# First stage of a four-layer network by groups: inputs, statistics and roots per group, rows turned one group ahead, two buffers of parts, first head's loads inside the stage

## The reference, cut to what matters

```python
xn = layernorm(x)                                   # no weights
q1, k1, q2, k2, v = split(xn @ Wqkv)                # 128, 128, 128, 128, 256 columns: 16 heads of 8 (v: 16)
lam = exp(lambda_q1 . lambda_k1) - exp(lambda_q2 . lambda_k2) + LAMBDA_INIT
diff = causal_softmax(q1, k1) @ v - lam * (causal_softmax(q2, k2) @ v)
x = x + layernorm(scaled_rms(diff) @ Wproj)
```

## Time and profile before

| | us |
|---|---|
| median of 3 runs | 1789.22 (1786.18 to 1791.82) |
| the profiled execution's own time | 1788.79 |
| its span, first to last instruction | 1787.0 |
| mean granted TensorE clock over the span | 0.943 |
| busy: PE, DVE, ACT, POOL | 1519.5, 1288.3, 1088.8, 1095.8 |

### The profile page before, as it was taken

One profiled execution on the slowest core, in us unless ns is written; L12 is line 12 of the kernel. 1 busy time (PEld: TensorE's weight loads), 2 busy tenths in 40 slices (PEclk: granted clock), 3 DMA queues, 4 the chain that ended last, 5 costly groups with the idle time before them and its releaser, 6 DMA issues. The chain is left out here.

```text
span 1787.0 us, 30008 instructions
## 1 busy us (share of the span) xinstructions
PE 1519.5 (85%) x8532; PEld 1025.8 (57%) x8532; DVE 1288.3 (72%) x3447; ACT 1088.8 (61%) x2348; POOL 1095.8 (61%) x1272
## 2 busy tenths in 40 slices
PE   3759999999999836468874899999999999988898
PEld 2413434344443315356653688888788888867565
DVE  5458887888888313755255899999999999983443
ACT  1105666676666721211312799999999999995242
POOL 5211565665647563104234699999999999974353
PEclk9958999999999968789986999999999999999899
DMA  3321011010100001762010000000000000000000
GB/s 118 113 64 36 22 26 29 19 36 18 30 24 20 2 1 47 246 225 95 1 47 0 1 1 2 1 1 1 1 1 1 29 21 1 1 1 1 1 24 24
DMA packets 39162, 59.48 MB, mean 33 GB/s; under 512 B 8700, under 2 KB 33160, under 8 KB 38152
## 3 DMA queue, kind: packets, MB, share of 16 engines
q1 hardware_dynamic: 39048, 58.12, 10.2%
HBM read 40.93 MB, written 16.78 MB: 32 GB/s over the span
## 5 line engine op out<-in xcount | busy, mean ns | idle before, releaser
L1896 POOL TENSOR_SCALAR c_R<-c_Z,c_negtau 128x256 f32<-128x256 f32 x519 | 589.7, 1167 | 51.4 <-DVE c_negtau L1965 29.7
L588 ACT ACTIVATE a_PT<-a_sc 128x512 f32<-128x512 f32 x576 | 318.4, 600 | 209.6 <-PE a_sc L653 207.2
L1851 ACT ACTIVATE c_R<-c_Z,c_negtau 128x256 f32<-128x256 f32 x1017 | 425.9, 517 | 3.5 <-DVE c_negtau L1998 1.8
L493 DVE TENSOR_REDUCE a_mpart<-a_nat 128x1 f32<-128x512 f32 (+3 forms) x640 | 364.0, 628 | 86.3 <-PE a_nat L620 48.1
L1932 DVE BATCH_NORM_STATS2 c_stat<-c_R 128x6 f32<-128x512 f32 x576 | 380.9, 678 | 1.7 <-ACT c_R L1851 1.6
L617 PE MATMUL a_nat<-KS,QS 96*128 96x512 bf16 (+3 forms) x768 | 242.4, 343 | 33.6 <-DMA KS<-qk_parts 23.8
L1768 PE MATMUL c_z<-mem,c_R 128*128 128x256 f32 x1024 | 231.5, 379 | 0.0
L653 PE MATMUL a_sc<-QS,KS 128*128 128x512 bf16 (+3 forms) x768 | 220.3, 330 | 8.3 <-ACT a_PT L588 5.7
L460 POOL TENSOR_SCALAR_AFFINE_SELECT a_PT<-a_PT 128x512 f32<-128x512 f32 x128 | 78.8, 639 | 223.2 <-ACT a_PT L588 223.2
L1768 PEld LDWEIGHTS c_z<-mem,c_R 128*128 128x128 f32 x1024 | 192.9, 190 | 25.4
L1925 DVE MAX8 c_x<-c_Z 128x8 f32<-128x256 f32 x384 | 152.3, 408 | 26.3 <-ACT c_Z L1839 25.8
(11 more groups left out here) (319 smaller groups left out, 2237.7 us busy)
## 6 DMA issues: line engine op xcount, KB each, us to landing
qk_parts<-a_parts SPq DMA_DIRECT2D x4, 1536.0 KB, 5.9
QS<-qk_parts SPq DMA_DIRECT2D x192, 32.0 KB
KS<-qk_parts SPq DMA_DIRECT2D x192, 32.0 KB
made<-m_made SPq DMA_DIRECT2D x24, 256.0 KB, 3.8
mem<-made SPq DMA_DIRECT2D x3, 2048.0 KB, 8.1
X<-in_L_attn_x_dram SPq DMA_DIRECT2D x1, 2048.0 KB, 8.4
ternary<-a_W_T SPq DMA_DIRECT2D x1, 2048.0 KB, 6.3
mem<-in_L_ffn_wq_dram SPq DMA_DIRECT2D x1, 2048.0 KB, 14.3
```

Source lines behind the costliest of these rows:

```text
L493: dve.tensor_reduce(mpart[:, b, j:j + cnt, i, k0 // 512], src, AX.X, ALU.max).then_inc(s_max, 1)
L588: act.activation(PT[:, n % 3, c, :], sc[:, u % 2, :], ACT.Exp, scale=SCALE0).then_inc(s_exp, 1)
L1851: act.activation(split(i, h) if r < NR else whole(i, h), Z[:, slot(i), h, :], ACT.Relu, bias=threshold(i, r, h)).then_inc(s_ra[r], 1)
L1896: pool.tensor_scalar(split(i, h) if r < NR else whole(i, h), Z[:, slot(i), h, :], threshold(i, r, h), 0.0, ALU.add, ALU.max).then_inc(s_rp ...
```

## The change

- **Inputs and statistics by group.** `X` is loaded by four DMAs of 512 KB, the first ahead of `w`, the other three behind it. VectorE takes the statistics of a group when that group has landed (`row_stats`), and GpSimd the roots of 4 tiles at a time (`root`).
- **Turned one group ahead.** PE's order becomes: turn group 0; then for each group the queries and keys, the turn of the next group, the values. `xT` has two buffers.
- **Two buffers of parts.** `parts` gets a second buffer; the waits for a store now go back two groups. The store of a group is four DMAs of 384 KB, one for each j, issued as soon as that j's low part is there. VectorE's order becomes `first_rest(j)`, `low(j - 1)`, and so on.
- **Work moved between engines.** The copy of the values to `VA` goes from VectorE to ScalarE. The memset of `QS` goes from VectorE to GpSimd. The chain for lam goes behind group 2.
- **GpSimd's memsets.** `VA` is set only in its 15 spare columns of 32 and the column of ones. `QS` and `KS` are set as fp32 words, 6144 in each partition in place of 12288 bf16. They stand between the roots and the casts: root of group 0, `QS`, root 1, casts of group 0, root 2, `KS[0:96]`, casts of group 1, root 3, `KS[96:128]`, casts of groups 2 and 3.
- **Early loads.** Between the stores of groups 1 and 2, SP waits for the stores of both groups (batch 0) and for the three memsets, and loads the batch 0 half of head 0, 24 DMAs of 16 KB. The second block then loads only the other half of head 0, and PE waits for that half at unit 20.
- **Loops written out.** The groups are no longer a hardware loop. `s_held` is no longer touched in this block. The wait for `w_proj` moves to the block that uses it.

The diff, cut to its core:

```diff
+def load_head(sp, K, n, buf, tokens, semaphore):
+    for j in range(2):
+        for side, (S, order) in enumerate(((K.QS, Q_PARTS), (K.KS, K_PARTS))):
+            for k, part in enumerate(order):
+                sp.dma_start(S[k * HD0:(k + 1) * HD0, buf, j, tokens],
+                             K.qk_parts[2 * j + side, part, ds(HD0 * n, HD0), tokens]).then_inc(semaphore, 16)
...
+            x = x_in.rearrange("b (t p) d -> p (b t) d", p=P)
+            sp.dma_start(X[:, rows(0), :], x[:, rows(0), :]).then_inc(s_x[0], 16)
             sp.dma_start(w[:], w_qkv_in.rearrange("(c p) n -> p c n", p=P)).then_inc(s_w, 16)
+            for g in range(1, NG):
+                sp.dma_start(X[:, rows(g), :], x[:, rows(g), :]).then_inc(s_x[g], 16)
             for n, v in enumerate(lam_in):
                 sp.dma_start(K.lam_in[:, n, :], v.rearrange("(a n) -> a n", a=1).broadcast_to([P, HD0])).then_inc(s_lam, 16)
+            sp.dma_start(K.w_proj[:], K.w_proj_in.rearrange("(c p) n -> p c n", p=P)).then_inc(K.s_w_proj, 16)
             load_ffn(sp, K, K.w_ffn)
+            for g in range(NG):
+                for j in range(4):
+                    sp.wait_ge(s_lo, 4 * g + j + 1)
+                    sp.dma_start(qk_parts[j].rearrange("s c t -> c s t")[:, :, g * GT * P:(g + 1) * GT * P],
+                                 parts[:, g % 2, j]).then_inc(s_parts[g % 2], 16)
+                if g == 1:
+                    for e in range(2):
+                        sp.wait_ge(s_parts[e], 16 * 4)
+                    sp.wait_ge(s_zero, 3)
+                    load_head(sp, K, 0, 0, slice(0, T), K.s_first)
+            for e in range(2):
+                sp.wait_ge(s_parts[e], 16 * 8)
...
+            pool.memset(VA[:, :, :, VD0 + 1:2 * VD0], 0.0).then_inc(s_pad, 1)
+            pool.memset(VA[:, :, :, VD0:VD0 + 1], 1.0).then_inc(s_pad, 1)
+            def root(g):
+                pool.wait_ge(s_mv, GT * g + GT)
+                pool.tensor_scalar(rstd[:, rows(g)], mv[:, rows(g), 1], LN_EPS, None, ALU.add).then_inc(s_var, 1)
+                pool.wait_ge(s_var, g + 1)
+                pool.tensor_tensor(rstd[:, rows(g)], rstd[:, rows(g)], K.mhalf[:, rows(g)], ALU.pow).then_inc(s_rstd, 1)
+            def middle(g):
                 for j in range(4):
+                    pool.wait_ge(s_rest, 4 * g + j + 1)
+                    if g >= 2:
+                        pool.wait_ge(s_parts[g % 2], 16 * 4)
+                    pool.tensor_copy(parts[:, g % 2, j, 1, :], rest[:, j, :]).then_inc(s_mid, 1)
+            root(0)
+            pool.memset(K.QS[:].bitcast(F32), 0.0).then_inc(s_zero, 1)
+            root(1)
+            middle(0)
+            root(2)
+            pool.wait_ge(s_rstd, 3)
+            pool.memset(K.KS[0:MROW].bitcast(F32), 0.0).then_inc(s_zero, 1)
+            pool.wait_ge(s_zero, 2)
+            middle(1)
+            root(3)
+            pool.wait_ge(s_rstd, 4)
+            pool.memset(K.KS[MROW:P].bitcast(F32), BF16_ONES).then_inc(s_zero, 1)
+            pool.wait_ge(s_zero, 3)
+            middle(2)
+            middle(3)
...
+            def row_stats(g):
+                dve.wait_ge(s_x[g], 16)
+                for k in range(GT):
+                    dve.bn_stats(stats[:, g * GT + k, :], X[:, g * GT + k, :]).then_inc(s_st, 1)
+                dve.wait_ge(s_st, GT * g + GT)
+                for k in range(GT):
+                    dve.bn_aggr(mv[:, g * GT + k, :], stats[:, g * GT + k, :]).then_inc(s_mv, 1)
             def normal(g):
+                dve.wait_ge(s_rstd, g + 1)
                 dve.wait_ge(s_turned, g)
                 for k in range(GT):
...
+            def first_rest(g, j):
+                dve.wait_ge(s_hi, 4 * g + j + 1)
+                if g > 0:
+                    dve.wait_ge(s_mid, 4 * (g - 1) + j + 1)
+                    dve.wait_ge(s_lo, 4 * (g - 1) + j + 1)
+                dve.tensor_tensor(rest[:, j, :], qk_ps[:, j, :], parts[:, g % 2, j, 0, :], ALU.subtract).then_inc(s_rest, 1)
+            def low(g, j):
+                dve.wait_ge(s_mid, 4 * g + j + 1)
+                dve.tensor_tensor(parts[:, g % 2, j, 2, :], rest[:, j, :], parts[:, g % 2, j, 1, :],
+                                  ALU.subtract).then_inc(s_lo, 1)
...
+            row_stats(0)
+            normal(0)
+            row_stats(1)
+            for g in range(NG):
+                if g + 1 < NG:
+                    normal(g + 1)
+                if g + 2 < NG:
+                    row_stats(g + 2)
                 for j in range(4):
+                    first_rest(g, j)
+                    if j > 0:
+                        low(g, j - 1)
+                low(g, 3)
+                if g == 2:
+                    factor()
...
+            copy_x(0)
+            for g in range(NG):
                 for j in range(4):
                     act.wait_ge(s_qk, 4 * g + j + 1)
+                    if g >= 2 and j == 0:
+                        act.wait_ge(s_parts[g % 2], 16 * 4)
+                    act.activation(parts[:, g % 2, j, 0, :], qk_ps[:, j, :], ACT.Copy).then_inc(s_hi, 1)
+                if g + 1 < NG:
+                    copy_x(g + 1)
+                act.wait_ge(s_v, g + 1)
+                act.activation(VA[:, rows(g), :, 0:VD0], v_ps[:].rearrange("p t (h d) -> p t h d", h=H0),
+                               ACT.Copy).then_inc(s_vc, 1)
+                if g == 2:
+                    act.wait_ge(s_lame, 1)
+                    act.activation(lam_s[:, 2:4], lam_s[:, 0:2], ACT.Exp).then_inc(s_lame, 1)
...
+            pe.wait_ge(s_ident, 3)
+            turn(0)
+            pe.wait_ge(s_w, 16)
+            for g in range(NG):
+                queries_keys(g)
+                if g + 1 < NG:
+                    turn(g + 1)
+                values(g)
...
-            load(Head(0, 0))
-            load(Head(0, 1))
+            load_head(sp, K, 0, 0, slice(T, B * T), s_load[0])
+            load_head(sp, K, 1, 1, slice(0, B * T), s_load[1])
...
-                if u == 0:
-                    pe.wait_ge(s_load[h.buf], 16 * LOADS * (h.times + 1))
+                head_0 = isinstance(h.n, int) and h.n == 0
+                if u == 0 and head_0:
+                    pe.wait_ge(K.s_first, 16 * HEAD_LOADS)
+                if u == (NU // 2 if head_0 else 0):
+                    pe.wait_ge(s_load[h.buf], 16 * HEAD_LOADS * (h.times + 1))
```

More of the change, by code:

```diff
@@ L133, in attention_inputs @@
-        s_hi, s_rest, s_mid, s_lo, s_vc = sem("a0_s_hi"), sem("a0_s_rest"), sem("a0_s_mid"), sem("a0_s_lo"), sem("a0_s_vc")
-        s_lamv, s_lame = sem("a0_s_lamv"), sem("a0_s_lame")
+        s_x = [sem(f"x{g}") for g in range(NG)]
+        s_parts = [sem(f"parts{e}") for e in range(2)]
+        (s_w, s_lam, s_ident, s_pool, s_pad, s_zero, s_st, s_mv, s_var, s_rstd, s_dve, s_xn, s_turned, s_xT, s_qk, s_v, s_hi, s_rest,
+         s_mid, s_lo, s_vc, s_lame) = (sem(n) for n in "w lam ident pool pad zero st mv var rstd dve xn turned xT qk v hi rest "
+                                       "mid lo vc lame".split())
@@ L162, in _ @@
             c.step(pool.memset(K.mask[:], 0.0))
-            c.step(pool.memset(mhalf[:], -0.5))
+            c.step(pool.memset(K.mhalf[:], -0.5))
             c.join()
@@ L182, in in_order @@
-            def in_order(g):
-                for j in range(4):
[L184 to L194, removed]
+            pool.memset(VA[:, :, :, VD0 + 1:2 * VD0], 0.0).then_inc(s_pad, 1)
@@ L196, in _ @@
+            middle(2)
+            middle(3)
+            pool.wait_ge(s_pad, 2)
+            pool.wait_ge(s_zero, 3)
         @block.vector
         def _(dve):
[L198 to L216, removed]
@@ L221, in normal @@
                 dve.wait_ge(s_turned, g)
                 for k in range(GT):
[L223 to L227, removed]
-                for j in range(4):
[L229 to L244, removed]
+                    t = g * GT + k
+                    dve.tensor_scalar(xn[:, k, :], X[:, t, :], mv[:, t, 0:1], rstd[:, t:t + 1], ALU.subtract,
+                                      ALU.mult).then_inc(s_xn, 1)
+            def first_rest(g, j):
[4 more added lines that the diff above has]
+                dve.tensor_tensor(rest[:, j, :], qk_ps[:, j, :], parts[:, g % 2, j, 0, :], ALU.subtract).then_inc(s_rest, 1)
@@ L366, in _ @@
         def _(sp):
-            def load(h):
-                for j in range(2):
-                    for side, (S, order) in enumerate(((QS, Q_PARTS), (KS, K_PARTS))):
-                        for n, part in enumerate(order):
-                            sp.dma_start(S[n * HD0:(n + 1) * HD0, h.buf, j, :],
-                                         qk_parts[2 * j + side, part, ds(HD0 * h.n, HD0), :]).then_inc(s_load[h.buf], 16)
             def maxima(h):
@@ L386, in period @@
                         hold(sp, s_sc, h.count(4 * NCH), K.s_held)
[L387 removed]
+                    later = h.next(2)
+                    load_head(sp, K, later.n, later.buf, slice(0, B * T), s_load[later.buf])
```

(2 more changed lines are left out.)

94 lines of the change are left out of this document (34 added, 60 removed).

## The result

The changed kernel takes 1776.33 us (median of 8 runs, 1774.42 to 1783.12); the kernel before takes 1792.23 us on the same chip. The ratio is 0.992, with an interval of 0.9903 to 0.9936: faster by 15.9 us, where 36.4 were forecast, and outside the range. The profiled execution took 1775.14 us for a span of 1773.4; before it was 1788.79 us for 1787.0, so these two differ by 13.6 us.

The account below looks back on a forecast made before the run. Waits in the first 107.4 us were taken as the bound: ScalarE's for stores, PE's 23.8 us for the first head. First head product moves from 107.4 to 71.0, so 1788.8 - 36.4 = 1752.4 us; range 1743 to 1760.

Parts of the forecast that it names:

- From 107.41 on the same work follows in the same order in both kernels: From the first product of the heads on: nothing changes, so its earlier start, 36.4 us, is the whole gain.
- Code written out instead of a loop: the last block is so written, and is the template used: First stage: groups written out instead of looped, costed at nothing.
- the sum: Step-by-step times of the first stage up to the first product of the heads at 71.0, for 1752.4 us in all.
- The price of a memset: Three GpSimd memsets of 6144 words behind the roots: each holds VectorE's normalizing 5.2 us, bounds 0 and 5.2.
- the near bound: GpSimd's setting of `VA` before the first root: 3.3 us at the plain memset's rate, against 7.9; taken as costing 0.
- The first rival: First stage: the memsets hold nothing, heads start at 63.8, gain 43.6 us, 1745.2 us; chance 0.20.
- Group 3's turn: Last turn of the first stage: PE waits for `normal(3)`, done at 51.0, so the turn ends at 51.3, not 50.3.
- Lows beside casts: First stage, VectorE's lows beside GpSimd's casts: each low held between 0 and 0.62 us; 1 us taken in all.
- the second rival: First stage: each low waits for a cast, VectorE and GpSimd become the bound; gain 31.3 us, 1757.5 us; chance 0.16.
- The slower rival: Heads: PE enters on another clock phase, partly at the 1.2 level; 1801 us at a share of 0.1; chance 0.02.
- the early loads' place in SP's queue: First block: 24 issues, 8.3 us, ahead of group 2's four stores, which wait up to 2 us; costed at nothing.
- head 0's second half: Start of second block: lands 10 us in, before VectorE reaches unit 20 at 12.2; costed at nothing.

Follow-up runs that it names:

- e2: 158 empty instructions at the head of TensorE's list in the kernel before, nothing else changed; 1810.88 us, ratio 1.0097.
- e1: 98 empty instructions (semaphore increments nobody waits for) at the head of TensorE's list in the changed kernel; 1754.74 us, ratio 0.979.
- e7: 60 empty instructions at the head of TensorE's list in the changed kernel; 1755.11 us.
- e8: 78 empty instructions at the head of TensorE's list in the changed kernel; 1751.57 us.
- e4: The changed kernel with GpSimd's three memsets of QS and KS issued behind the normalizing instead of behind the root; 1771.13 us, ratio 0.9884.
- e12: The changed kernel with 78 empty TensorE instructions and no early loads, head 0 loaded whole in the second block; 1761.58 us, ratio 0.9834.
- e3: 256 empty instructions at the head of TensorE's list in the changed kernel; 1803.05 us, ratio 1.0053.
- e5: 100 empty instructions at the head of TensorE's list in the kernel before; 1806.31 us.
- e9: The changed kernel with the loop over heads written out on every engine, 16 heads one after the other; 1753.23 us, ratio 0.9781.
- e10: The changed kernel with the loop over heads written out and GpSimd's three memsets behind the normalizing; 1746.31 us, ratio 0.9742.

## Why the prediction was wrong

**The step that failed** is "From 107.41 on the same work follows in the same order in both kernels", and with it "Code written out instead of a loop: the last block is so written, and is the template used", costed at nothing. The work is the same, but TensorE's instructions lie elsewhere. The distance from the first `a_nat` to the end, which I said would be 1679.6 us within 3, is 1700.8 (1773.4 - 72.59): 21.2 us more. e2 shows the loss without the rest of the change (17.4 us by the medians, 22 between the profiled executions), e1, e7 and e8 show the change without it: 1751.57 to 1755.11 us, around the forecast of 1752.4, and 1674.9 to 1680.6 us from the first `a_nat` to the end. That 1752.4 is met so closely is in part luck: the sum starts from an execution of 1788.79 us, and against the kernel before of their own rounds these three gain 38.8 to 43.0 us, not 36.4.

**Point by point, the first stage.** Statistics 5.28 (5.3 forecast), roots done at 8.55 (8.6), memset over at 13.73 (13.8), first query product at 17.16 (17.4). The price of a memset (5.2 us each) held in all three places, and `VA` took 3.30 us, the near bound. By the Trainium skill, "SBUF — State Buffer", section "Who interferes with whom", the loser of the shared port pair is blocked for the whole instruction; the 6.24 us of four instructions that take 1.38 in e4 agree. The first rival, free memsets, was wrong; e4 comes near to what it would have brought, and it is less than its sum (4.5 us, not 7.2), since the stores end late next.

**Group 3's turn** was to make PE late by 1.0 us. PE waited 2.25 us for it, having been 1.1 us ahead of the sum until then (48.3 against 49.4), and the wait had a second price that I left out: the clock. Over the 3.95 us behind it the granted clock was 0.58. From the first transpose to the next query product went 6.18 us (50.55 to 56.73), where the sum had 0.87 + 3.45 = 4.32: 1.86 us, more than the whole miss of 1.6 at the first head product. The last 16 products ended at 63.76 instead of 61.6 (62.6 with the collisions), the last low at 66.91 instead of 65.4. Landing and change of blocks took 5.7 us, as summed. First head product 72.59 against 71.0.

**Lows beside casts.** I allowed the low to be held. It is the cast that is: 1.01 us beside a low, 0.61 alone, as two rows of GpSimd in the last group show. VectorE and GpSimd never became the bound, so the second rival was wrong too.

```profile
60.08 0.61 POOL L198 CAST a_parts<-a_rest 128x512 bf16<-128x512 f32 x1 [3.41 <-DVE a_rest L241]
61.75 1.01 POOL L198 CAST a_parts<-a_rest 128x512 bf16<-128x512 f32 x1 [1.05 <-DVE a_rest L241]
```

**The slower rival** put a loss in the heads and gave the clock as its cause. Half right: the loss is there, and the clock does stand at 0.50 for some us at each jump back. But it falls behind a gap of 2.8 us in which PE waited for nothing that the profile shows, and where that gap is gone (e1) it stays at 1.00. So the clock makes the loss larger and is not its start.

**What was costed at nothing and is nothing:** the early loads' place in SP's queue (dear only once the memsets are late, e4), head 0's second half (after the change the first `a_sc` comes 34.8 us earlier, as does the first `a_nat`), the buffers, the lam chain.

**Open:** which instructions stay loaded and where the limits lie; which engine's instructions each packet brings (the filler stands in TensorE's list alone, and the gaps are TensorE's, but the queue's rows name no engine); why the part behind the last power takes 1126.3 to 1126.5 us in three kernels (e1, e8, e12), 1129.2 to 1130.2 in seven, and 1131.5 to 1134.2 in four (e3, e5, e9, e10). Each of these is one execution, and the executions of one kernel differ by up to 9 us, so that this last difference may mean nothing.

## What to carry to other kernels

Code ahead of a loop is not free for the loop: a change in the number of instructions of the busiest engine can shift a long loop so that each jump back costs 3 to 8 us, in lines that the diff doesn't touch. When a gain of the first stage is lost later, compare one event per pass of the loop in both traces, then look for idle time put down to "issue" and for packets on the instruction queue; write the loop out, or shift it by a few instructions, before you judge the change. And a GpSimd memset belongs behind the normalizing that waits for the same root, not ahead of it.

## What the runs showed of the hardware

- A loop of 1653 TensorE instructions costs nothing at its jump back in some places (31.5 us for that head) and 3 to 8 us in others, with 80 or 81 instead of 52 or 53 packets of 16 KB on the instruction queue; written out, it is fetched all along (16 packets in 276 us) without a stall. In the slow place 8 or 9 packets come in every pass, so about the whole loop is fetched again (6.46 blocks of 256, at some 250 instructions to a packet, an estimate).
- An empty semaphore increment costs TensorE 0.154 us: 256 of them put the first transpose at 40.35, 98 at 15.97.
- A GpSimd memset of 6144 words (5.2 us) holds VectorE's normalizing instructions beside it: four take 6.24 to 6.35 us, and 1.38 without it. A cast of GpSimd beside a `low` is itself held, 1.01 us instead of 0.61.
- Two gaps of 2 to 3 us in PE were followed by several us at or near the 1.2 level (0.51 from 232 to 239 us, 0.58 from 50.55 to 54.50), so that these waits cost half to nearly once as much again.
